# One decoder layer on one core: the first shared group's gate and up products moved from the expert part into the last iterations of the attention

## The reference

```python
x = layernorm(x + differential_attention(x))
x = layernorm(x + cross_attention(x, ctx, ctx))
x = layernorm(x + moe(x))
```

```python
def moe(x, w_router, wg, wu, wd, sg, su, sd):   # 8 experts, top 2, hidden 640; 2 shared experts
    xt = x.reshape(-1, 256)                      # 2048 tokens
    scores = sigmoid(xt @ w_router.T)
    topk_w, topk_i = top_k(scores, 2)            # weights divided by their sum
    routed = sum over the 2 experts i of topk_w * ((silu(xt @ wg[i].T) * (xt @ wu[i].T)) @ wd[i].T)
    shared = sum over the 2 shared experts of (silu(xt @ sg.T) * (xt @ su.T)) @ sd.T
    return routed + shared
```

## Time and profile before

| | |
|---|---|
| median of 3 runs | 864.04 us (863.94 to 866.16) |
| the profiled execution | 862.43 us |
| its span, first to last instruction | 860.2 us |
| PE busy | 783.0 us, 91% |
| DVE busy | 521.6 us, 61% |
| ACT busy | 519.4 us, 60% |
| POOL busy | 313.6 us, 36% |
| expert part begins | 447.25 us |

### The profile page before, as it was taken

How to read it: one execution, slowest core, us unless ns; L and a number is a source line. 1 busy time by engine, 2 the same in 40 slices (tenths; PEclk the granted TensorE clock), 3 DMA queues, 4 the chain that set the end, 5 groups by cost and what they waited for, 6 DMA issues and landing times. The chain is left out here.

```text
span 860.2 us, 19949 instructions
## 1 busy us (share of the span) xinstructions
PE 783.0 (91%) x7605; PEld 512.2 (60%) x7605; DVE 521.6 (61%) x1182; ACT 519.4 (60%) x942; POOL 313.6 (36%) x481
## 2 busy tenths in 40 slices
PE   6888899999999999988869999999999999999993
PEld 5444555555555555555435555557788888887652
DVE  3454677888888888875426876664444444444353
ACT  2444578888888888875444555544555556555443
POOL 3133344555555555545220386001222222222222
PEclk9787699999999999997559999999999999999998
DMA  8219000000000000000003587331332323232331
GB/s 242 64 49 254 2 2 2 2 2 3 2 2 2 2 2 3 2 2 1 2 11 128 174 239 255 106 128 39 49 51 44 50 45 51 45 49 45 52 109 61
DMA packets 38281, 51.00 MB, mean 59 GB/s; under 512 B 9264, under 2 KB 33072, under 8 KB 38192
## 3 DMA queue, kind: packets, MB, share of 16 engines
q1 hardware_dynamic: 31040, 40.39, 15.9%
q0 software_dynamic: 7152, 9.34, 6.6%
HBM read 31.04 MB, written 18.68 MB: 58 GB/s over the span
## 5 line engine op out<-in xcount | busy, mean ns | idle before, releaser
L1360 POOL DMA_INDIRECT acc<-y_sb,xin x39 | 60.5, 1552 | 217.5 <-ACT y_sb L1428 217.5
L1681 PE MATMUL ps<-wr,xr_hi 128*128 x624 | 129.3, 299 | 0.0
L1399 ACT ACTIVATE th<-ps 128x384 f32<-128x384 f32 (+1 forms) x118 | 58.0, 491 | 108.4 <-PE ps L1681 103.5
L1681 PE MATMUL ps<-xg_hi,wsh 128*128 128x512 f16 x320 | 102.5, 382 | 4.8 <-DVE xg_lo L1546 4.8
L676 DVE TENSOR_REDUCE c_qs<-ps 128x4 f16<-128x512 f32 x128 | 84.4, 694 | 32.0 <-PE ps L934 30.4
L676 DVE TENSOR_REDUCE a_qs<-ps 128x4 f16<-128x512 f32 x128 | 85.3, 691 | 23.7 <-PE ps L934 22.8
L509 ACT ACTIVATE a_pt<-ps 128x512 f32<-128x512 f32 x128 | 74.5, 596 | 36.3 <-PE ps L951 34.4
L1681 PE MATMUL ps<-wr,xr_lo 128*128 x312 | 93.4, 299 | 0.0
L1553 DVE SCALAR_TENSOR_TENSOR th<-th,ps 128x384 f32<-128x384 f32 (+1 forms) x118 | 65.3, 553 | 33.4 <-ACT th L1399 33.2
L509 ACT ACTIVATE c_pt<-ps 128x512 f32<-128x512 f32 x128 | 69.7, 602 | 20.0 <-PE ps L951 19.6
L1640 DVE COPY ht<-ps 128x512 f16<-128x512 f16 x39 | 16.6, 425 | 94.0 <-PE ps L1760 94.0
(11 more groups left out here) (211 smaller groups left out, 1762.9 us busy)
## 6 DMA issues: line engine op xcount, KB each, us to landing
wst<-in_wx SPq DMA_DIRECT2D x30, 640.0 KB, 4.6
xs<-zero SPq DMA_DIRECT2D x1, 5031.0 KB, 24.7
xin<-xs SPq DMA_DIRECT2D x39, 129.0 KB, 2.1
acc<-x_row SPq DMA_DIRECT2D x4, 512.0 KB, 3.2
x_row<-acc SPq DMA_DIRECT2D x8, 256.0 KB, 5.0
out<-x_row SPq DMA_DIRECT2D x8, 256.0 KB, 2.1
x_row<-in_x SPq DMA_DIRECT2D x1, 1536.0 KB, 10.6
wst<-in_wqkvT SPq DMA_DIRECT2D x1, 768.0 KB, 4.3
```

What stands on the lines that cost most here:

```text
L1360: pool.indirect_dma_start(acc, bass.IndirectOffsetOnAxis(ap=row, axis=0), y_sb[:, n % 2, :], None, compute_op=ALU.add).then_inc(f_acc, 16)
L1399: act.activation(th[:, k % 2, 0:n], gate[:, k % 2, 0:n], ACT.Silu, scale=1.0 / WSCALE).then_inc(f_th, 1)
L1681: ins = pe.matmul(o, l[x], r[y], start=(first and n == 0), stop=(last and n == m - 1), skip_group_check=not (first and last))
```

## The change

**Units in the attention.** Group 0's gate and up products, their Silu, gating and splitting are done in iterations 17 to 21 of the attention. A table `SPARE` puts 23 places there, up to seven per iteration: two that turn and split 256 tokens each, 20 units, each for one chunk of 128 hidden features and 256 tokens, and one for the last low part. A unit is 12 products of 256 columns into bank 4 on PE, a Silu on ACT, the gating on DVE, the high part on ACT and the low part on DVE at the next place. All units use the one bank, so a unit's products wait for the gating of the one before.

**The result's place.** The hidden values, high and low, stay in `hold`, which lies where the last four of the 24 routed weight pieces (20 to 23) will lie. Before ACT splits piece 20 it waits for the end of group 0's down products.

**The expert part.** Group 0 has only its 120 down products left, with the rank products of the routing between them after step 8. The routing runs in one go on DVE with the first four pieces between its parts; slots and tile numbers follow in group 1's first two steps. Groups 1 and 2 take one piece in each of their 10 steps. The rank products go to another bank, and group 1's second step waits for DVE to have read it.

**The start.** The shared weights are split half a piece per iteration: ACT in iterations 3 to 14 ahead of the last copy of the body, DVE in iterations 5 to 16 behind the body. The `keep_warm` behind `restack` in iterations 1 and 2 sends 16 products, not 8. SP's clearing of `xs` comes ahead of the shared weights' pieces 2 to 5. In the final normalisation four semaphores become one.

```diff
+SPARE = {key: k for k, key in enumerate(
+    [(17, p) for p in (3, 4, 5, 6, 7)] + [(n, p) for n in (18, 19) for p in (1, 2, 3, 4, 5, 6, 7)]
+    + [(20, p) for p in (3, 5, 7)] + [(21, 5)])}
...
+        hold = sb("hold", [P, 2, STEPS, GT], F16)
...
 # ACT, body(n)
+                k, half = divmod(n - SHARED_HIGH, 2)
+                if 0 <= k < NSH * 3:
+                    split_high(act, 0, k, wsh[:, k // 3, k % 3, 0, :], half)
                 if live(n - 1):
                     reqt_in(A, a_one, n - 1)
+                spare(n, 7)
...
-                if n <= NSH * 3 // 2:
-                    for k in range(2):
-                        e, m = divmod(2 * n - 2 + k, 3)
-                        split_high(act, n - 1, k, wsh[:, e, m, 0, :])
 # DVE
+            def pre_gated(u):
+                dve.wait_ge(p_act, u + 3)
+                dve.scalar_tensor_tensor(out=pre_h[:, u % 2, :], in0=pre_h[:, u % 2, :], scalar=1.0 / WSCALE,
+                                         in1=a_one[:, GT // 2:], op0=ALU.mult, op1=ALU.mult).then_inc(p_dve, 1)
...
 # PE
+            def pre_up(u):
+                if u == 0:
+                    pe.wait_ge(s_xwlo, 3 * NSH)
+                pe.wait_ge(p_dve, u + 2)
+                e, j = u % STEPS // IC, u % IC
+                for m in range(2):
+                    n = 0
+                    for c in range(EC):
+                        at = slice(c * I + j * P, c * I + (j + 1) * P)
+                        for l, x in ((0, pre_hi), (0, pre_lo), (1, pre_hi)):
+                            ins = pe.matmul(a_one[:, m * GT // 2:(m + 1) * GT // 2], wsh[:, e, m, l, at],
+                                            x[:, c, unit_rows(u)], start=(n == 0), stop=(n == 3 * EC - 1))
+                            n += 1
+                ins.then_inc(p_pe, 1)
...
                 if 1 <= n < 3:
-                    keep_warm(8)
+                    keep_warm(16)
...
 # experts: ACT
+            def piece_high(q):
+                if q == HOLD:
+                    act.wait_ge(f_gdown, 1)
+                split_high(act, 0, NSH * 3 + q, wr[:, q, 0, :])
...
 # experts: PE
-            group_T(0)
-            pe.wait_ge(f_nought, 1)
-            for g in range(EG):
-                group(g, rank_at=None if g else 3)
+            group_T(1)
+            pe.wait_ge(f_nought, 2)
+            for s in range(STEPS):
+                group_down(0, None, s)
+                if s == RANK_AT:
+                    rank_products()
+            for g in range(1, EG):
+                group(g)
```

## The result

The changed kernel takes 877.67 us (median of four runs, 876.08 to 880.00), the kernel before 864.43 beside it (863.94 to 866.16): a ratio of 1.0152, with an interval of 1.0124 to 1.0179. It is slower by 13.2 us; the forecast was 875, in 850 to 899. The profiled execution of the changed kernel is the longest of its four, 880.00 us with a span of 877.8.

A forecast was written before the change was run, and what follows sets the result against it. Settled iterations were taken as PE's, with the clock below full at both attention ends. Tail +42, expert part -21, start -10.5 and settled iterations +0.5 gave +11 on 862.43, so 873.4 us, 875 as a median, range 850 to 899.

The forecast's parts named there:

- The tail, +42 forecast: Attention iterations 17 to 22: units and table loads added there cost +42 us, with ends +10 and +59.
- the 35.4: Stretches with loads in iterations 17 to 19: ACT gets 35.4 us more work, 3 absorbed by idle time, leaving +32.5.
- I take **+6** for both: Heads of iterations 18 and 19: three units each through one PSUM bank, +6 us for both heads (0 to +12).
- the +1.5: End of the attention: last three units beside the last batches' normalisation, whose statistics wait behind one gating, +1.5 us (0 to 8).
- the tail looks as if it had room: Iterations 17 to 22: ACT busy 30.97 of 65.42 us, PE 17.96 of 20.52 in iteration 18, 13.32 of 16.73 in 19.
- The long waits stand at the heads of the iterations, where no load is: Attention's last iterations: ACT's long waits (7.51 us before iteration 19's first exps) cannot hide any of the 21 loads.
- The expert part, -21 forecast: Expert part: -28 us until group 1's first down product, partly given back later; -21 in all, ends -16 and -25.
- The start, -10.5 forecast: Iterations 1 to 4: -4.5 us from shorter waits less added warming products, -6 from the clock; -10.5 in all.
- I take one of the three: Start: one of three half-clock stretches returns to full clock, -6 us, between 0 and -19.5.
- Settled iterations, +0.5 forecast: Iterations 3 to 16: half a weight piece split in each fits ACT's and DVE's waits, +0.5 us; 18 without that cover.
- Full clock at both ends: Rival, chance 0.29: clock holds 2.4 GHz in iterations 2 to 4 and 18 to 19; sum -11.5, so 852.5 us.
- A load holds ACT longer than its row: Rival, chance 0.11: each of 21 table switches on ACT takes 1.3 us more, +27, so 902 us.

The follow-up runs named there:

- the start's part alone: Kernel before with only shared-weight splitting moved to later iterations, 16 warming products for 8 and earlier clearing of `xs`; no units, old expert part: 847.41 us, ratio 0.9848.
- the two Tanh kernels: Changed kernel with Silu computed through Tanh: in its own gating order 857.96 us (ratio 0.9967), with DVE's gating one place later 876.06 us (1.02).
- the later gating: Changed kernel with DVE's gating of a unit, and the high and low parts behind it, one place later: 893.25 us, ratio 1.0429.

## Why the prediction was right, and where its terms were off

**The sign and the size** came out, 875 for 877.67, and the closeness is partly luck. The sum stood on three terms, and against the profiled executions they were off by +9.7, +3.1 and -6.2 us; the settled iterations by another -0.5, and the rest of the program by +0.5. So a forecast of +11 met +17.6 there, and +13.2 in the medians. Within the tail the terms were off by more.

**The tail, +42 forecast, +51.7 measured.** The total's ends (+10 to +59) held it; the split inside was wrong. By stage, before and after:

| | before | after | difference |
|---|---|---|---|
| iteration 17 | 19.1 | 26.8 | +7.7 |
| heads of 18 and 19 | 10.0, 8.3 | 20.9, 19.8 | +22.4 |
| from the first exps on, 18 and 19 | 10.5, 8.5 | 18.0, 16.5 | +15.5 |
| iterations 20 to 22 | 9.1 | 15.2 | +6.1 |

A head holds four units: the three that the forecast priced by themselves, and ahead of them the one of the last place of the iteration before, which it counted among the 35.4. The run without units at the first three places of 18 and 19 tells them apart:

| term | forecast | measured |
|---|---|---|
| three units each at the heads of 18 and 19 | +6 | 13.4 |
| the other units of 17 to 19 with all loads, and the transposes | +32.5 + 2 | 32.2, as what is left |
| iterations 20 to 22, with the last three units and the one of 19's last place | +1.5 | +6.1 |

The step that failed is "I take **+6** for both", and beside it the +1.5: nine units at 7.5 us, which is to say hidden for the most part beside other work. The pieces of a unit were right (1.3, 0.38 and 0.42 us); the overlap was not. The six units at the heads took 2.2 us each, and iterations 20 to 22 four times what was counted. Behind it stands the reading "the tail looks as if it had room". PE was busy 52.09 of 65.42 us there, but the 13.3 us left over were not where the units went. The heads of 18 and 19 by themselves, before and after:

```profile
400.93:410.92 9.99, 9.40 (x74) 6.08 (x70) 7.61 (x16) 1.59 (x4) 4.61 (x10) 0.50 0.01 2
421.45:429.70 8.25, 6.66 (x66) 4.45 (x62) 6.56 (x13) 0.60 (x1) 2.88 (x5) 0.71 0.01 2
...
391.99:412.84 20.85, 17.66 (x130) 12.79 (x127) 10.44 (x25) 6.52 (x13) 3.59 (x6) 0.65 0.01 2
430.88:450.63 19.75, 15.90 (x122) 11.60 (x119) 9.42 (x21) 5.63 (x10) 2.99 (x5) 0.67 0.00 1
```

PE was already busy 16.1 of the 18.2 us. Nor did the clock become full there, by which PE's part of the old work was to shrink: it is 0.65 and 0.67, where it was 0.50 and 0.71. The 240 products of all units are 26 us at full clock. The forecast named those 26 us as an argument for the rival with the full clock and gave them no term of its own. The run with four products in a unit shows that they lie on the path: eight of twelve products are 18.1 us. Taken out in this order, the loads are 23.5 us, those products 18.1, and 10.1 for the last four products, the copies, the gating and the splitting make up the 51.7; in another order the shares may differ.

The loads' own price was near: 27 us counted, 23.5 measured by taking them out. "The long waits stand at the heads of the iterations, where no load is" was misread: three of the 21 loads stand ahead of the first Silu in the heads of 18 and 19 and in iteration 20, and behind them ACT waits 3.17, 2.58 and 3.54 us for that unit's products. Those three cost nothing of their own there; the other 18 are 23.1 us. The agreement with 23.5 is in part chance, as the clock has its share in that number.

**The expert part, -21 forecast, -17.9 measured.** The chain of the first pieces was right within 1 us (26.5 against 27.4). Mis-sized were the returns behind it (-28 and the 7.5 that were counted for them make -20.5, not -21). On ACT, from group 1's first Silu to group 2's first it takes 48.7 us instead of 42.6, and from there to the first routed tile's 48.1 instead of 44.1: 10.1 us given back, where 7.5 were counted. The wait of 4.41 us for the last piece, before it was 1.50, is the end of that. So this part lost 120 products of 512 columns, 25.8 us by the prediction's 0.215, and is 17.9 us shorter; the tail took 28.2 more without any load. Per unit that is 1.4 us paid for 0.9 won, and so taking the loads out doesn't make the units win.

**The start, -10.5 forecast, -16.7 measured** (with the settled iterations; -12.9 in the trace of the start's part alone). The step that failed is "I take one of the three": both first half-clock stretches went, the third stayed, as the argument against the rival had it. Its reason, waits that the change leaves, is not shown: in iteration 4 the 3.91 us wait of the earlier trace rows is gone, and no PE wait there exceeds 0.78. The 1.4 counted for the added warming products was not seen: with and without them the kernel takes the same time.

**Settled iterations, +0.5 forecast.** Iterations 5 to 15 take 22.22 to 22.25 us in both kernels. The cover in the earlier trace rows held.

**The rivals.** *Full clock at both ends* was right on the start (16.7 of its 24 us) and wrong on the tail: the mean clock there rose from 0.68 to 0.79, but the heads did not become free. *A load holds ACT longer than its row* is refuted by the rows of iteration 18: with its data there, the exp behind the load that ends at 412.83 starts at 412.84, and a Silu at 415.54 behind one that ends at 415.53. The Trainium skill's 2.66 us for a switch, load and drain ("ScalarE: Activation LUTs", section "What ACT_TABLE_LOAD costs") differs from that: here a switch is 1.3 us between two instructions, and taking 21 out gave 1.12 us for each. The section "Table sets: the hidden batching unit" of the same page of the Trainium skill names tanh beside exp in one set; the two Tanh kernels agree, with 2 loads in the program instead of 24, and in the change's own order the tail is 20.2 us shorter.

**Other signs named beforehand.** 24 loads: seen. ACT busy some 75 in the tail: 73.2. Tail 100 to 112 us: 117.1, and 115.1 when run again. Iterations 18 and 19 near 32 and 29: 38.9 and 36.2, by the heads. Iterations 2 to 4 near 22 us each, a sign against the forecast: 21.3 and 20.9 us, but 26.9 in iteration 4.

## What to carry to other kernels

Work that is moved into a stretch that "has room" has to be counted on every engine that it uses and at the place where it goes, not only on the engine with the visible new cost: here the loads on ACT took the eye, and 26 us of products cost about as much, because PE's 13.3 us of idle time lay for the most part elsewhere (2.2 us of it at the heads); after the change PE was idle for 31.8 us of the tail. Where a function is wanted among activations of another set, look for a formula in the set that is loaded: half of g times (1 + tanh) made this kernel's tail 20 us shorter, without its loads, for one DVE instruction more per unit. And a change of several parts is worth taking apart: the splitting of the shared weights, moved out of the first iterations, won 1.6% by itself.

## What was not expected of the hardware

The granted clock of a stretch rose where waits were taken away, with no product added. With the splitting moved and the 8 warming products of before, iterations 2 and 3 have a mean clock of 1.00 where it was 0.75, and take 20.9 us each instead of 27.5 and 27.6. Sixteen warming products with all the waits left in place give iteration 2 a clock of 1.00 too, at 22.1 us. Either was enough in iteration 2, and the two together gave no more. With the splitting moved alone PE's busy time in iterations 2 and 3 fell by 5.5 and 6.1 us, about half of the 12 to 14 us of PE work in such a half-clock stretch, as the forecast had worked it out for one.

Taking a wait from one engine's queue to another's can cost more than the wait: the later gating ran the same instructions in another order, and the tail went from 115.1 to 127.3 us.
